# A projection kernel's result stores, and one load, moved from GpSimd's DMA queue to SyncE's

## The chip, the cores and the metric

The kernel runs as one program on the 8 cores of one Trainium2 chip. Each core takes 2048 of the 16384 tokens and works alone; nothing is exchanged. The metric is the device time in microseconds of the slowest core, from the runs of one kernel on one chip.

## The reference, cut to what matters

```python
x = x + layernorm(attn(layernorm(x)))       # x: 16384 tokens x 4096, float32
x = x + layernorm(ffn(layernorm(x)))

# attn, token by token: q, k, v are 64 heads x 64
q, k, v = x @ Wq.T, x @ Wk.T, x @ Wv.T      # q, k, v scaled by sigmoid masks
w = softmax(einsum('bshd,bsgd->bshg', q, k) / 8)    # heads against heads of one token
attn = einsum('bshg,bsgd->bshd', w, v).reshape(b, s, 4096) @ Wo.T

# ffn: a 4096x4096 base projection, and a top-2-of-8 LoRA of rank 16
ffn = x @ W_base.T + b_base + 2 * sum over the two chosen e of w_e * (x @ A_e.T) @ B_e.T
```

## The kernel before, in words

A core handles its tokens in two chunks of 1024 (`c` = 0, 1), each of 8 tiles (`tau`) of 128 tokens. One buffer in SBUF, `LNT`, holds the chunk transposed; the five 4096x4096 products (wq, wk, wv, wo, wb) all take their stationary operand from it and stream the weights through four buffers `WG0` to `WG3`.

One weight group is 512 rows by 512 columns in bf16 (512 KB), so a product has 8 column blocks `n` of 8 groups `ktg` each. `load_wgroup` (L240) fetches a group. The first time a weight is used (`cast_save`: in chunk 0, for wq, wk, wv and for the first half of wo and of wb) GpSimd issues the load from the float32 weight, cast on the way (`WG<-woT`, L247), and SyncE then issues a store of the bf16 group to a scratch tensor (`s_wo<-WG`, L250); the buffer is free for the next load when that store has landed and TensorE is done with it. Every later time (`scratch`) SyncE issues a plain load of the bf16 group (`WG<-s_wo`, L253). All of these run through the helper `dma` at L147/L148, so the trace gives them the line L148.

The stages of a chunk, in the order in which they are written out:

1. Layernorm of the 8 tiles and their transposes into `LNT` (`transpose_tile`, L278, evicted at L290 and L292).
2. q, k and v (L325 to L370): for each `n` 64 groups of matmuls into 8 banks (L343), then 8 evictions (L355, L361) and 8 stores of 128 KB from `QST` to `qn`, `kn`, `vn`, issued by SyncE.
3. Attention (`attn_batch`, L375): a tile is two batches; each gathers q, k, v in pieces of 128 bytes by 8 DMAs of SyncE (`QSG<-qn`, `KB<-kn`, `VB<-vn`), computes, and stores `OB` to `on` by 2 DMAs of SyncE (L537). After both batches of a tile, `a3_units` (L544) loads the tile of `on` into `BFN` (L549) and transposes it into `LNT`. Tiles 0 to 3 are done with all 8 banks before the projection begins.
4. wo, in two halves (`proj_half`, L575): tiles 0 to 3 in banks 0 to 3, with the attention of tiles 4 to 7 as a generator that is advanced three units after each group; then tiles 4 to 7, with the post-attention layernorm and the router (`a5_b0_units`, L619) of tiles 0 to 3. After each `n`, 4 evictions by ScalarE into the four slots of `APST` (L603) and 4 stores of 256 KB to `apn` (L607).
5. wb, in two halves (`b1_half`, L745): the same form, with a bias matmul (L778) and a LoRA matmul (L782) at the end of each `n`, 4 evictions (L787) and 4 stores to `yn` (L791). The final layernorm of tiles 0 to 3 (`b6_units`, L804) stands between the halves, that of tiles 4 to 7 at the end.

Nothing schedules this at run time: `emit` (L121) appends each instruction with its waits to the list of its engine, and each engine works through its list in order. So a DMA that must wait holds back whatever stands behind it on the engine that issues it. With four `WG` buffers, the load of group `ktg` waits for the matmuls of the group four before it.

Of the kernel before, what the change touches and what calls it, by code (L numbers as in the profile page):

```python
# [26 lines left out]
def _build_program():  # L27
# [24 lines left out]
    on_d = nc.dram_tensor("on", [CH, DM], BF16, kind="Internal").ap()  # L52
    ap_d = nc.dram_tensor("apn", [CH, DM], F32, kind="Internal").ap()
    yn_d = nc.dram_tensor("yn", [CH, DM], F32, kind="Internal").ap()
# [18 lines left out]
    BFN = sb("BFN", [128, DM], BF16)  # L73
# [73 lines left out]
    def dma(eng, out, in_, waits=(), sem=None):  # L147
        return emit(eng, lambda e, o=out, i=in_: e.dma_start(out=o, in_=i),  # L148
                    waits, inc=sem, amt=16)
# [147 lines left out]
    for c in range(NCH):  # L297
      try:
# [2 lines left out]
        src_kind0 = "cast_save" if c == 0 else "scratch"  # L301

        ph(1, c)
        lnt_rdy = {}
        for tau in range(TAU):
            xbuf, bname = (XT, "XT") if tau % 2 == 0 else (T2, "T2")
            lw = g_w(bname)
            if c == 0 and tau == 0:
                lw += [("setq", 48), ("G", g0)]
            qsem = "xl" if tau % 2 == 0 else "t2l"  # L310
            uq = dma("gpsimd", xbuf[:], x_d[row0 + tau * 128: row0 + tau * 128 + 128, :], lw,
                     sem=qsem)
            av = lnorm(xbuf[:], BFN[:], [(qsem, uq)] + g_w("BFN"))
            g_set(bname, ("V", av))
            fw = [("V", av)] + (g_w("LNTa", "LNTb") if tau == 0 else [])
            vv, ss = transpose_tile(BFN, lambda kt, tau=tau: colk(kt, tau), fw)
            lnt_rdy[tau] = [("V", vv), ("S", ss)]
            g_set("BFN", ("T", cnt["T"]))
        a1_v, a1_s = cnt["V"], cnt["S"]

# [4 lines left out]
        for nm in ("wq", "wk", "wv"):  # L325
            for n in range(NB):
                for ktg in range(8):
                    b, rdy = load_wgroup(nm, n, ktg, src_kind0)
                    for k4 in range(4):
                        kt = ktg * 4 + k4  # L330
                        for tau in range(TAU):
                            waits = []
                            if k4 == 0 and tau == 0:
                                waits.append(rdy)
                            if ktg == 0 and k4 == 0:
                                waits += g_w(f"bank{tau}")
                                if nm == "wq" and n == 0:
                                    waits += lnt_rdy[tau]
                            last = (ktg == 7 and k4 == 3)
                            emit("tensor",  # L340
                                 lambda e, kt=kt, tau=tau, b=b, k4=k4,
                                        st=(ktg == 0 and k4 == 0), sp=last:
                                 e.matmul(pb(tau, 0, 512),  # L343
                                          LNT[:, colk(kt, tau):colk(kt, tau) + 128],
                                          WG[b][:, k4 * 512:k4 * 512 + 512],
                                          start=st, stop=sp),
                                 waits, inc="T" if (k4 == 3 and tau == TAU - 1) else None)
                    wg_done(b, "T", cnt["T"])
# [195 lines left out]
        def a3_units(taus, wavesz, banks):  # L544
            for tau in taus:
                for bt in range(2):
                    yield from attn_batch(tau, bt, wavesz, banks)
                on_q = [("ob0", cnt["ob0"]), ("ob1", cnt["ob1"])]
                uq = dma("gpsimd", BFN[:], on_d[tau * 128:tau * 128 + 128, :],  # L549
                         list(on_q) + g_w("BFN"), sem="onr")  # L550
                lnt_key = "LNTa" if tau < 4 else "LNTb"
                fw = [("onr", uq)] + (g_w(lnt_key) if tau % 4 == 0 else [])
                yield
                transpose_tile(BFN, lambda kt, tau=tau: colk(kt, tau), fw, banks=banks)
                g_set("BFN", ("T", cnt["T"]))
                yield
# [18 lines left out]
        def proj_half(nm, taus, banks, src, gen, img_d, first_waits=()):  # L575
            for n in range(NB):
# [23 lines left out]
                for ti, tau in enumerate(taus):  # L600
                    sl = ap_i[0] % 4
                    ap_i[0] += 1
                    ev = emit("scalar", lambda e, bk=banks[ti], sl=sl: e.activation(  # L603
                        APST[:, sl * 512:sl * 512 + 512], pb(bk, 0, 512), AF.Copy),
                        ([("T", tmm)] if ti == 0 else []) + g_w(f"APs{sl}"), inc="S")
                    g_set(f"bank{banks[ti]}", ("S", ev))
                    uv = dma("gpsimd", img_d[tau * 128:tau * 128 + 128, 512 * n:512 * n + 512],  # L607
                             APST[:, sl * 512:sl * 512 + 512], [("S", ev)], sem=f"ap{sl}")
                    g_set(f"APs{sl}", (f"ap{sl}", uv))

# [134 lines left out]
        def b1_half(taus, banks, src, gen):  # L745
            for n in range(NB):
# [28 lines left out]
                for ti, tau in enumerate(taus):  # L775
# [12 lines left out]
                        APST[:, sl * 512:sl * 512 + 512], pb(bk, 0, 512), AF.Copy),  # L788
                        [("T", tmm)] + g_w(f"APs{sl}"), inc="S")
                    g_set(f"bank{banks[ti]}", ("S", ev))  # L790
                    uv = dma("gpsimd", yn_d[tau * 128:tau * 128 + 128, 512 * n:512 * n + 512],  # L791
                             APST[:, sl * 512:sl * 512 + 512], [("S", ev)], sem=f"ap{sl}")
                    g_set(f"APs{sl}", (f"ap{sl}", uv))
                g_set(f"bfTn{bfb}", ("T", cnt["T"]))
# [87 lines left out]
```

How the kernel before makes its waits and increments, by code:

```python
        def run(eng):  # L828
            for waits, fn, inc, amt in sched[name]:
                for s_, v_ in waits:
                    eng.wait_ge(sems[s_], v_)
                instr = fn(eng)
                if inc is not None:
                    instr.then_inc(sems[inc], amt)
```

## Time and profile before

| | us |
|---|---|
| runs of the kernel before | 8191.3, 8231.3, 8757.5 |
| median | 8231.3 |
| the profiled execution, device time | 8199.5 |
| its span, slowest core (core 1) | 8197.9 |
| spans of all cores | 8128.0 to 8197.9 |
| TensorE matmuls busy (core 1) | 5404.7 (66%) |
| weight loads busy | 2558.1 (31%) |
| VectorE busy | 1492.1 (18%) |
| ScalarE busy | 774.8 (9%) |
| GpSimd busy | 496.2 (6%) |
| DMA queue of GpSimd (q0), share of 16 engines | 26.8% |
| DMA queue of SyncE (q1), share of 16 engines | 23.3% |

The rows below are of core 1, in microseconds from the start of its span. Of the stages, chunk 0's q, k and v lie at about 130 to 1710, its attention and wo at 1710 to 3225, wb and the final layernorm at 3225 to 4250; chunk 1 has q, k and v at 4361 to about 5990, attention and wo to 7323, wb to 8079. A profile's row gives the busy time of a group of instructions and, in brackets, the idle time of the engine just before it with what ended it.

### The profile page before, as it was taken

What the parts mean: (1) busy time and instruction counts of PE and PEld (TensorE: products, weight loads), DVE (VectorE), ACT (ScalarE), POOL (GpSimd) and SP (SyncE); (2) the same over time, 40 slices, a digit from 0 to 9 for tenths busy, and PEclk for the clock granted to TensorE, in tenths of its full rate; (3) what the DMA queues carried; (4) which work ended last, traced back from release to release, by engine and by line L of the source; (5) the groups of instructions that cost most, each with busy time, mean ns of one, the idle gap of its engine ahead of it and who ended that gap; (6) DMA issues with size and microseconds to landing.
All of it is one profiled execution on the core that took longest, in us unless ns stands there. A gap on an engine that the chain in (4) does not pass through costs nothing.

```text
span 8197.9 us, 69969 instructions; the slowest of 8 cores (8128.0 to 8197.9 us)
## 1 busy us (share of the span) xinstructions
PE 5404.7 (66%) x28056; PEld 2558.1 (31%) x28056; DVE 1492.1 (18%) x2144; ACT 774.8 (9%) x1427; POOL 496.2 (6%) x785
## 2 busy tenths in 40 slices
PE   4888888842345457564917888888832565576864
PEld 2333333322222223221313333333322332233321
DVE  4000000023212251302042000000023222513012
ACT  1000000012112210000001000000012222100000
POOL 1000000000001000110100000000000000000010
PEclk7999999965677778787958999999965787788987
DMA  6666666632566655798552222222222443555655
GB/s 149 141 144 144 142 144 140 141 80 52 95 141 130 134 191 185 170 188 231 171 203 85 77 77 78 78 77 78 77 54 52 113 107 102 194 190 157 202 183 191
DMA packets 940079, 1084.79 MB, mean 132 GB/s; under 512 B 575217, under 2 KB 792306, under 8 KB 923378
## 3 DMA queue, kind: packets, MB, share of 16 engines
q0 software_dynamic: 225872, 492.98, 26.8%
q1 hardware_dynamic: 713890, 587.34, 23.3%
q8 instruction: 229, 3.75, 0.2%
q14 instruction: 88, 0.72, 0.0%
HBM read 885.23 MB, written 369.10 MB: 153 GB/s over the span
## 4 chain that ended last, share of the span: by engine, by line
PE 59%; DMA 15%; DVE 11%; ACT 6%; SPq 5%; issue 3%; POOL 1%; DVEq 0%; ACTq 0%; POOLq 0%
PE PALL L343 33%; PE PALL L592 11%; PE PALL L765 8%; SPq L148 5%; DVE BN L192 4%; DMA T<-yn 3%; DMA WG<-wbT 3%; ACT QBD L496 2%; ACT PSTG L472 2%; DMA VB<-vn 1%; PE PALL L278 1%; DMA WG<-woT 1%; PE PALL L489 1%; PE PALL L409 1%; DMA T<-apn 1%
## 5 line engine op out<-in xcount | busy, mean ns | idle before, releaser
L343 PE MATMUL PALL<-WG,LNT 128*128 128x512 bf16 x12288 | 2795.8, 389 | 407.9 <-DVE QST L361 109.3
L343 PEld LDWEIGHTS PALL<-WG,LNT 128*128 128x128 bf16 x12288 | 1224.2, 100 | 1978.8 <-issue 614.7
L592 PE MATMUL PALL<-WG,LNT 128*128 128x512 bf16 x4096 | 1034.3, 413 | 175.9 <-DMA WG<-woT 89.6
L765 PE MATMUL PALL<-WG,LNT 128*128 128x512 bf16 x4096 | 949.5, 393 | 133.9 <-DMA WG<-wbT 119.4
L278 PE MATMUL PALL<-idt,BFN 128*128 128x128 bf16 x1536 | 168.3, 307 | 825.2 <-DVE BFN L204 616.5
L592 PEld LDWEIGHTS PALL<-WG,LNT 128*128 128x128 bf16 x4096 | 418.9, 105 | 733.1 <-issue 355.3
L765 PEld LDWEIGHTS PALL<-WG,LNT 128*128 128x128 bf16 x4096 | 407.8, 101 | 663.0 <-issue 230.2
L192 DVE BATCH_NORM_STATS2 BN<-T 128x6 f32<-128x512 f32 x320 | 193.5, 675 | 1739.3 <-DMA T<-yn 1285.0
L361 DVE TENSOR_TENSOR QST<-PALL,maskK 128x512 bf16<-128x512 f32 x128 | 81.0, 684 | 2059.5 <-PE PALL L343 2017.0
L278 PEld LDWEIGHTS PALL<-idt,BFN 128*128 128x128 bf16 x1536 | 158.2, 145 | 840.2 <-issue 840.2
L437 ACT ACTIVATE KTS<-PALL 128x512 bf16<-128x512 f32 x192 | 104.2, 594 | 3048.1 <-PE PALL L429 3048.1
L409 PE MATMUL PALL<-idt,QSG 128*128 128x128 bf16 x1024 | 104.2, 273 | 328.7 <-DMA VB<-vn 321.5
L418 DVE CAST QBD<-PALL 128x512 bf16<-128x512 f32 x256 | 161.9, 684 | 745.8 <-PE PALL L409 745.8
L361 DVE TENSOR_TENSOR QST<-PALL,maskV 128x512 bf16<-128x512 f32 x128 | 80.9, 684 | 992.1 <-PE PALL L343 955.3
L489 PE MATMUL PALL<-idt,PSTG 128*128 128x128 bf16 x1024 | 101.8, 269 | 241.7 <-ACT PSTG L472 241.7
L409 PEld LDWEIGHTS PALL<-idt,QSG 128*128 128x128 bf16 x1024 | 89.4, 125 | 348.9 <-issue 337.8
L472 ACT ACTIVATE PSTG<-PALL,NM 64x512 bf16<-64x512 f32 x256 | 167.8, 679 | 285.0 <-DVE NM L466 162.4
L483 DVE TENSOR_REDUCE ZW<-PSTG 128x8 f32<-128x1024 bf16 (+1 forms) x96 | 151.2, 1575 | 199.9 <-ACT PSTG L472 199.9
L290 DVE CAST LNT<-PALL 128x512 bf16<-128x512 f32 x192 | 132.7, 691 | 272.2 <-PE PALL L278 271.8
L778 PE MATMUL PALL<-bbn,onesb 1*128 1x512 bf16 x128 | 51.4, 401 | 194.8 <-DMA bbn<-bb 194.8
L787 ACT ACTIVATE APST<-PALL 128x512 f32<-128x512 f32 x128 | 76.2, 597 | 1049.2 <-PE PALL L782 1045.2
L148 POOL DMA_DIRECT2D BFN<-on x16 | 8.6, 536 | 2702.9 <-DMA on<-OB 2702.9
(99 smaller groups left out, 2149.3 us busy)
## 6 DMA issues: line engine op xcount, KB each, us to landing
WG<-s_wo SPq DMA_DIRECT2D x192, 512.0 KB, 3.3
WG<-s_wb SPq DMA_DIRECT2D x192, 512.0 KB, 3.7
XT<-x POOLq DMA_DIRECT2D x24, 2048.0 KB, 11.6
WG<-wqT POOLq DMA_DIRECT2D x64, 512.0 KB, 5.9
s_wq<-WG SPq DMA_DIRECT2D x64, 512.0 KB, 3.6
WG<-wkT POOLq DMA_DIRECT2D x64, 512.0 KB, 5.6
s_wk<-WG SPq DMA_DIRECT2D x64, 512.0 KB, 3.1
WG<-wvT POOLq DMA_DIRECT2D x64, 512.0 KB, 5.7
```

The costliest lines, as they stand in the source:

```text
L148: return emit(eng, lambda e, o=out, i=in_: e.dma_start(out=o, in_=i), waits, inc=sem, amt=16)
L192: emit("vector", lambda e, i=i: e.bn_stats(BN[:, 6 * i:6 * i + 6], src_ap[:, 512 * i:512 * i + 512]), (list(vwaits) + g_w("MV") + g_w("BN" ...
L278: emit("tensor", lambda e, bk=bk, kt=kt, off=off: e.matmul(pb(bk, off * 128, 128), src_sb[:, kt * 128:kt * 128 + 128], idt[:], start=True, ...
L343: e.matmul(pb(tau, 0, 512), LNT[:, colk(kt, tau):colk(kt, tau) + 128], WG[b][:, k4 * 512:k4 * 512 + 512], start=st, stop=sp),
L361: ev = emit("vector", lambda e, tau=tau, sl=sl, mk=mk: e.tensor_tensor(QST[:, sl * 512:sl * 512 + 512].rearrange("p (h d) -> p h d", d=64) ...
L409: emit("tensor", lambda e, j=j, jj=jj, p=p, qb_bk=qb_bk: e.matmul(pb(qb_bk[j // 4], (j % 4) * 128, 128), QSG[p][:, jj * 128:jj * 128 + 128 ...
L418: emit("vector", lambda e, pw=pw, bk=bk, i_=i_: e.tensor_copy(QBD[pw][:, i_ * 512:i_ * 512 + 512], pb(bk, 0, 512)), [("T", t_s0)] if i_ == ...
L472: s_s6 = emit("scalar", lambda e, a=a, pw=pw, bk_i=bk_i, sb_=s_bk[bk_i]: e.activation(PSTG[pw][64 * a:64 * a + 64, bk_i * 1024:bk_i * 1024 ...
L489: emit("tensor", lambda e, j=j, pw=pw, ptb=pt_bk[j // 4], po=(j % 4) * 128: e.matmul(pb(ptb, po, 128), PSTG[pw][:, j * 128:j * 128 + 128], ...
L496: emit("scalar", lambda e, pw=pw, bk=bk, i_=i_: e.activation(QBD[pw][:, i_ * 512:i_ * 512 + 512], pb(bk, 0, 512), AF.Copy), [("T", t_s7)] ...
L592: e.matmul(pb(bk, 0, 512), LNT[:, colk(kt, tau):colk(kt, tau) + 128], WG[b][:, k4 * 512:k4 * 512 + 512], start=st, stop=sp),
L765: e.matmul(pb(bk, 0, 512), LNT[:, colk(kt, tau):colk(kt, tau) + 128], WG[b][:, k4 * 512:k4 * 512 + 512], start=st, stop=False), waits,
```

## The change

It has three parts.

- The load `BFN<-on` (L549; 16 of them), the stores `apn<-APST` (L607; 128) and the stores `yn<-APST` (L791; 128) are issued by SyncE and no longer by GpSimd.
- Their waits stay as they are, and so do sizes, buffers and semaphores.
- The first matmuls of wq in a chunk no longer wait tile by tile for the evictions of that tile's transposes; the matmul of tile 0 waits once, for all of them.

```diff
-            vv, ss = transpose_tile(BFN, lambda kt, tau=tau: colk(kt, tau), fw)
-            lnt_rdy[tau] = [("V", vv), ("S", ss)]
+            transpose_tile(BFN, lambda kt, tau=tau: colk(kt, tau), fw)
...
-                                if nm == "wq" and n == 0:
-                                    waits += lnt_rdy[tau]
+                                if nm == "wq" and n == 0 and tau == 0:
+                                    waits += [("V", a1_v), ("S", a1_s)]
...
-                uq = dma("gpsimd", BFN[:], on_d[tau * 128:tau * 128 + 128, :],
+                uq = dma("sync", BFN[:], on_d[tau * 128:tau * 128 + 128, :],
                          list(on_q) + g_w("BFN"), sem="onr")
...
-                    uv = dma("gpsimd", img_d[tau * 128:tau * 128 + 128, 512 * n:512 * n + 512],
+                    uv = dma("sync", img_d[tau * 128:tau * 128 + 128, 512 * n:512 * n + 512],
                              APST[:, sl * 512:sl * 512 + 512], [("S", ev)], sem=f"ap{sl}")
...
-                    uv = dma("gpsimd", yn_d[tau * 128:tau * 128 + 128, 512 * n:512 * n + 512],
+                    uv = dma("sync", yn_d[tau * 128:tau * 128 + 128, 512 * n:512 * n + 512],
                              APST[:, sl * 512:sl * 512 + 512], [("S", ev)], sem=f"ap{sl}")
```

On SyncE (SP), where chunk 0 goes from the first half of wo to the second, the order before was (`WG<-s_wo` is a load of a bf16 weight group, `apn<-APST` a store of results):

```order
L148 DMA s_wo<-WG 128x2048
L148 DMA on<-OB 64x32x64 x2
L148 DMA WG<-s_wo 128x2048 x64
L148 DMA s_wb<-WG 128x2048 x64
L148 DMA WG<-s_wb 128x2048 x64
```

and the same place of SyncE after the change is:

```order
L148 DMA s_wo<-WG 128x2048
L148 DMA apn<-APST 128x512 x4
L148 DMA on<-OB 64x32x64 x2
L148 DMA BFN<-on 128x4096
L148 DMA WG<-s_wo 128x2048 x8
L148 DMA apn<-APST 128x512 x4
L148 DMA WG<-s_wo 128x2048 x8
L148 DMA apn<-APST 128x512 x4
```

The 64 loads of a half now stand in eights, with the four stores of the block just computed between one eight and the next.

On GpSimd (POOL), from chunk 0's attention to its second column blocks of wo, the order before was (`WG<-woT` is the load of a float32 weight group with a cast):

```order
L148 DMA WG<-wvT 128x4x512 x64
L148 DMA BFN<-on 128x4096 x4
L148 DMA WG<-woT 128x4x512 x8
L148 DMA apn<-APST 128x512 x4
L148 DMA WG<-woT 128x4x512 x8
L148 DMA apn<-APST 128x512 x4
L148 DMA WG<-woT 128x4x512 x2
L148 DMA BFN<-on 128x4096
```

and after the change:

```order
L148 DMA WG<-wvT 128x4x512 x64
L148 DMA WG<-woT 128x4x512 x64
L148 DMA T<-apn 128x4096
L148 DMA XT<-x 128x4096
L148 DMA xp<-XT 128x4096
```

The 64 casting loads of the half now follow one another with nothing between them.

On SyncE, around the first tile boundary of the attention that is interleaved with chunk 0's wo (`QSG`, `KB`, `VB` are the gathers of the next batch), the order before was:

```order
L148 DMA on<-OB 64x32x64 x2
L148 DMA s_wo<-WG 128x2048
L148 DMA QSG<-qn 64x32x64 x2
L148 DMA KB<-kn 64x16x64 x4
L148 DMA VB<-vn 64x32x64 x2
L148 DMA s_wo<-WG 128x2048 x8
```

and after the change:

```order
L148 DMA on<-OB 64x32x64 x2
L148 DMA BFN<-on 128x4096
L148 DMA s_wo<-WG 128x2048
L148 DMA QSG<-qn 64x32x64 x2
L148 DMA KB<-kn 64x16x64 x4
L148 DMA VB<-vn 64x32x64 x2
L148 DMA s_wo<-WG 128x2048 x7
L148 DMA apn<-APST 128x512 x4
```

The load of `BFN`, which waits for the two stores of `OB` to land, now stands ahead of the next batch's gathers.

## Rows read from the trace of the kernel before

**Rows 1.** Spans and granted TensorE clock by core

```profile
core 1: 8197.9 us, clock 0.812
```

**Rows 2.** Who waited for whom: us in total, times, longest us

```profile
PE PALL L778 <- DMA bbn<-bb: 194.8, 2, 97.6
...
PE PALL L765 <- DMA WG<-wbT: 119.4, 37, 14.2
...
PE PALL L592 <- DMA WG<-woT: 89.6, 10, 12.9
PE PALL L343 <- DMA WG<-s_wv: 84.1, 8, 11.6
PE PALL L343 <- DMA WG<-s_wk: 82.8, 8, 11.7
...
PE PALL L343 <- DMA WG<-s_wq: 70.9, 7, 11.0
```

**Rows 3.** Timeline, chunk 1's wq, one block to the next: start, us, engine

```profile
4418.21 4.37 SPq L148 DMA_DIRECT2D qn<-QST  x8
...
4422.67 1.84 SPq L148 DMA_DIRECT2D WG<-s_wq  x4
4427.04 3.57 PE L343 MATMUL PALL<-WG,LNT 128*128 128x512 bf16 x8 [9.66 <-DMA WG<-s_wq]
```

**Rows 4.** Stretch behind it: us, PE, PEld, DVE, ACT, POOL busy, PEclk, DMA share, GB/s

```profile
4427.00:4430.40 3.40, 3.36 (x8) 1.24 (x9) 0.00 (x0) 0.00 (x0) 0.00 (x0) 0.50 0.82 333
```

**Rows 5.** Timeline, chunk 0's second half of wo, one block to the next

```profile
3046.80 2.07 ACT L603 ACTIVATE APST<-PALL 128x512 f32<-128x512 f32 x4 [28.90 <-PE PALL L592]
...
3047.54 4.65 PE L592 MATMUL PALL<-WG,LNT 128*128 128x512 bf16 x17 [0.89 <-ACT APST L603]
```

**Rows 6.** Timeline, chunk 1's first half of wb, one block to the next

```profile
7543.64 2.52 ACT L787 ACTIVATE APST<-PALL 128x512 f32<-128x512 f32 x4 [28.07 <-PE PALL L782]
```
```profile
7545.02 0.39 PE L782 MATMUL PALL<-bfTn,HWT 128*128 128x512 bf16 x1
...
7546.30 27.14 PE L765 MATMUL PALL<-WG,LNT 128*128 128x512 bf16 x125 [0.25 <-ACT APST L787]
```

**Rows 7.** Timeline, chunk 0's first half of wo, block 0 to 1

```profile
2222.10 3.02 POOL L148 DMA_DIRECT2D WG<-woT  x4
```

**Rows 8.** The same block boundary, TensorE's own timeline

```profile
2231.45 9.29 PE L592 MATMUL PALL<-WG,LNT 128*128 128x512 bf16 x32 [12.79 <-DMA WG<-woT]
```

**Rows 9.** Busy time and DMA, chunk 0's first half of wb (columns of rows 4)

```profile
3484.00:3772.00 288.00, 201.25 (x816) 81.26 (x814) 0.00 (x0) 13.36 (x23) 49.56 (x75) 0.86 0.93 195
```
```profile
3505.00:3510.00 5.00, 4.38 (x22) 1.82 (x20) 0.00 (x0) 0.00 (x0) 0.00 (x0) 1.00 1.12 246
```

**Rows 10.** Timeline, chunk 0's attention, tile 0 to tile 1, three engines

```profile
1815.04 3.96 SPq L148 DMA_DIRECT2D QSG<-qn  x2
```
```profile
1818.96 0.54 POOL L148 DMA_DIRECT2D BFN<-on  x1 [133.67 <-DMA on<-OB]
```
```profile
1833.08 1.78 PE L409 MATMUL PALL<-idt,QSG 128*128 128x128 bf16 x16 [3.53 <-DMA VB<-vn]
```

**Rows 11.** Timeline, chunk 0, tile 3's attention into wo, SyncE and TensorE

```profile
2117.29 1.70 SPq L148 DMA_DIRECT2D on<-OB  x2
...
2135.81 8.31 SPq L148 DMA_DIRECT2D QSG<-qn  x2
```
```profile
2162.43 1.01 PE L409 MATMUL PALL<-idt,QSG 128*128 128x128 bf16 x8 [21.36 <-DMA VB<-vn]
```

**Rows 12.** DMA issues between 2858 and 2880 us: KB each, median us to landing

```profile
BFN<-on POOLq DMA_DIRECT2D x1, 1024.0 KB, 10.7
```

**Rows 13.** DMA issues of the whole span (columns of rows 12)

```profile
WG<-s_wo SPq DMA_DIRECT2D x192, 512.0 KB, 3.3
```

**Rows 14.** Timeline, chunk 0, the last transposes' evictions and the first matmuls of wq

```profile
128.42 4.81 PE L343 MATMUL PALL<-WG,LNT 128*128 128x512 bf16 x18
128.72 0.59 ACT L292 CAST LNT<-PALL 128x512 bf16<-128x512 f32 x1 [0.27 <-PE PALL L278]
```

More of the change, by code:

```diff
@@ L303, in _build_program @@
         ph(1, c)
-        lnt_rdy = {}
         for tau in range(TAU):
```

## The prediction

> **What bounds the kernel now.** I began with the cores: all lie within 1%, and core 1 is the slowest [rows 1], so one core's queues tell the story. Its two totals of waits came next [rows 2]. The reader should see two things there. TensorE waits for scratch weights only in wq, wk and wv (70.9 + 82.8 + 84.1 = 237.8 us in 23 times, 10.3 us each): there the result stores already stand on SyncE ahead of the next loads. And in chunk 0 it waits for the casting loads of wo (89.6 us in 10 times) and wb (119.4 us in 37), where the stores stand on GpSimd ahead of the casting loads. Idle time of GpSimd and SyncE themselves costs nothing and I left it aside. Then I read the timeline at one boundary of each kind. TensorE with its weights bounds every projection, so the question at each block boundary (column block n to n+1) is which queue holds the next weights back.
>
> The change swaps the sides. Scratch projections of wo and wb, which today run through the boundary, get the stop that wq, wk and wv show; the two casting halves lose theirs.
>
> **Cost 1: block boundaries on scratch weights.** Today wo loses 0.89 us at a boundary [rows 5], and about 0.8 us more while three further banks are evicted at 0.5 us under matmuls of 0.22; wb loses 0.25 us [rows 6]. Afterwards SyncE reaches the next eight loads only after the last eviction and four stores. For wo the evictions run 2.07 us from 0.15 us after the last matmul [rows 5] and the last store takes about 0.5 us to issue (4.37 us for 8 [rows 3]), so the load is issued at 2.8 us. For wb the evictions keep pace with the L782 matmuls and end at 7546.16 [rows 6], 0.75 us after the last one ends at 7545.41: load issued at 1.3 us.
>
> From the first load's issue to the restart takes 4.4 us at the boundary of rows 3 (4422.67 to 4427.04). Its gap of 9.66 is 0.7 short of the mean of 23, which puts the leg at 5.0 on average. Here 1 MB of stores is in the queue within 2 us, not within 4.4, so I allow up to 1.5 more and take 0.5. The gap becomes 8.3 us in wo and 6.8 in wb; less what is lost today (1.7 and 0.25) that is 6.6 us each. Then the clock: behind the stop of rows 3 the eight matmuls take 3.57 us, with the granted clock at 0.50, its level of 1.2 GHz [rows 4]; at 2.4 GHz they take 8 x 0.217 (27.14 us for 125 [rows 6]) = 1.7. That adds 1.8 (3.57 less 1.74), so 8.4 us a boundary; I take 8.3, for a leg sometimes as short as in rows 3.
>
> Such boundaries: 7 in each of five half-products (wo second half and wb second half in both chunks, wb first half in chunk 1) = 35, x 8.3 = 290 us. Low end: the first load lands as fast as one in mid-block, 3.3 us [rows 13], with nothing ahead of it: 6.1 us a boundary (213 in all). High end: it waits for the whole megabyte, 3.1 us at the 333 GB/s of rows 4 less the 0.5 from last store to load, a leg of 7.6: 10.5 us (368). In chunk 1's first half of wo there are 7 more, but with attention in between TensorE is at half clock much of the time, so only the gap counts: 7 x 6.6 = 46 (35 to 60).
>
> The changes of half are hidden: behind wb's first half TensorE stands 97 us for `bbn<-bb`, which GpSimd reaches after the final layernorm [rows 2], and the weights are in long before. If that cover were gone, two more boundaries, 17 us.
>
> Where the load stands against the stores is weighed once more. In rows 3 a megabyte of stores was issued ahead of the load and it still started TensorE after 4.4 us. The Trainium skill ("DMA: Bandwidth & Descriptors", section Queues, rings and completion order) says that each DMA engine takes the descriptors of one issuing engine's ring in order, and alternates between the rings of two; by that rule the load, now in the stores' ring, waits for all that is left of them. By the row the sum has 290 us here, by the rule it would have 368. No row has stores of this size ahead of a load.
>
> **Cost 2: `BFN<-on` on SyncE.** Behind it stand the next batch's gathers. They are issued at 1815.04; `on` is seen as landed at 1818.96 [rows 10], so they start 4 us later, plus the load's own 1 MB, which already shares the engines today. TensorE waits 3.53 us for the gathers already. I take 3 us for each of 6 tile boundaries in the pure attention, 18 in all (6 to 30), and 19 for four in chunk 1's interleaved part (6 to 25), where the gathers today come just in time.
>
> **Cost 3: the single wait.** TensorE starts at 128.42, the last eviction ends at 128.72 + 0.59 = 129.31 [rows 14]: 1 us a chunk, 2 us.
>
> **Gain 1: chunk 0's first half of wo.** GpSimd issues `WG<-woT` at 2222.10, after evictions and stores, and TensorE restarts after 12.79 us [rows 7, 8]. Of the ten waits of rows 2 seven are of this kind and three short, so about 12.4 each. With the queue freed they fall to some 0.9: 7 x 11.5 = 80 us. SyncE's copy to scratch is then late by a few us, but its buffer is only needed four groups later (some 25 us with the attention between). Moreover the gathers of the next tile stand on SyncE behind `s_wo<-WG`, which waits for a casting load that GpSimd issues only after `BFN<-on`: they go out at 2135.81, 18.5 us after the stores of `OB` at 2117.29 [rows 11]. Now they go 6 us after them, and no longer beside four casting loads. That takes most of the 21.36 us gap, and 17, 11 and 7 at the next three tiles by the same reading: 56 together. 80 + 56 = 136; the casting loads now compete with the gathers inside the blocks, for which I take off 15: 121 us (80 to 136).
>
> **Gain 2: chunk 0's first half of wb.** The same order, but the DMA engines are busy 0.93 of the time [rows 9]. The 816 matmuls of those 288 us are six blocks of 136, 48 us each, with 44.6 us of DMA work. Packed as tightly as a full stretch (1.12 [rows 9]) it would take 40; I take 6.4 us a block, 45 in all (0 to 90, the latter if nearly the whole stop went, 7 x 12.8 as in rows 8).
>
> **Gain 3: end of the attention.** At 2860 `BFN<-on` needs 10.7 us [rows 12] because 4 MB of `T<-apn` and `XT<-x` are issued with it; these go out earlier now. 6 us a chunk, 12 (0 to 16).
>
> **Sum.** 290 + 46 + 18 + 19 + 2 - 121 - 45 - 12 = +197 us on the profiled execution's 8199.5: 8397 us, or 2.4% slower. That execution lies between the two lower runs (8191.3 and 8231.3), so it is a fair base.
>
> **Rivals.**
> - *Chunk 0 pays it back.* The casting halves lose their stops wholly and the scratch stops are short: cost 213 + 35 + 12 + 2 = 262, gain 136 + 90 + 16 = 242, so 8220 us, no slower. The place is GpSimd's queue in chunk 0. It decides from a gain of 213 us on, where the middle costs (375) leave 162 us, under 2%. For it: stops of 12 to 13 us are longer than those that arise. Against: there are 14 of them against 42, and rows 9 leave little DMA time in wb.
> - *The queue does not matter.* The loads and stores use the same engines whoever issues them; then only 272 issues move, none of which any engine waits for, and the time stays at 8200 us. Against it stand the 23 stops of wq, wk and wv, in the same form. The Trainium skill states this rule ("DMA: Bandwidth & Descriptors", section Issuing engines are not separate DMA queues: issuing from several engines saves only the sequencer's time to initiate); it says nothing of a wait ahead in the queue.
> - *Stores and loads collide.* The leg from issue to restart grows to 7 us or more because 1 MB of float32 is ahead on the same queue: 10.5 us a boundary, 368 + 60, and the gains fall to 150 as the casting halves get the same collisions: 8199.5 + 428 + 39 - 150 = 8517 us. For it: the stores are twice the size of those in rows 3. Against: the DMA engines have room even behind the restart, 0.82 [rows 4].
>
> **How the numbers follow.** My forecast has 0.55, chunk 0 paying back 0.20, the neutral queue 0.08, the collision 0.17. Two per cent (164 us) is about what a measurement of this kernel can tell from no change. The forecast's own spread reaches below 8364 about one time in ten (0.05 of its 0.55); slower is 0.50 + 0.17 = 0.67. The first two rivals are within 2% but for 0.04 of faster, should the tile boundaries in chunk 0 gain twice what I read: same is 0.05 + 0.16 + 0.08 = 0.29. The range runs from 8280, well into the first rival, to 8530, just over the third.
>
> **What would show it.** In the changed kernel's waits L592 and L765 should wait for `WG<-s_wo` and `WG<-s_wb` some 42 times at 7 to 8 us, and SyncE for ScalarE's `APST`. The waits of L592 for `WG<-woT` should nearly vanish, those of L765 for `WG<-wbT` shrink by a third, and the gap before L409 at chunk 0's tile 4 fall from 21 us to a few. Chunk 1 should lose about 240 us and chunk 0 gain about 45. It is wrong if L592 and L765 run through the scratch boundaries, or if chunk 0 gains over 210 us.

## The result, and the profile after

The changed kernel took 8654.2 us in the median of 10 runs, the kernel before 8402.1 us in 10 runs on the same chip. The ratio is 1.0262, 95% interval 1.0232 to 1.0291: slower, by 2.6% where 2.4% was forecast. Some executions of either kernel have the cores of one die at a lower granted clock and take several per cent longer, which the ratio leaves out and the medians don't; cores 0 to 3 of the profiled execution after are such cores, so core 5 is read here, in both traces. The forecast of 8397 us, and its range up to 8530, lie below the median of 8654.2. Spans and clock of the changed kernel:

```profile
core 1: 8499.3 us, clock 0.795
...
core 5: 8404.2 us, clock 0.807
```

and the kernel before, the same core:

```profile
core 5: 8167.1 us, clock 0.814
```

That is 237 us more, 2.9% of this core's span. TensorE's waits of the changed kernel (us in total, times, longest):

```profile
PE PALL L590 <- DMA WG<-s_wo: 216.2, 28, 15.7
...
PE PALL L763 <- DMA WG<-s_wb: 168.6, 25, 8.9
...
PE PALL L763 <- DMA WG<-wbT: 73.7, 40, 5.0
```

and the same of the kernel before, core 5, which answer to [rows 2]:

```profile
PE PALL L765 <- DMA WG<-wbT: 120.7, 37, 14.4
...
PE PALL L592 <- DMA WG<-woT: 87.7, 9, 13.1
...
PE PALL L592 <- DMA WG<-s_wo: 60.0, 8, 16.1
...
PE PALL L765 <- DMA WG<-s_wb: 8.1, 4, 2.8
```

(Lines behind the first edit stand two lower after the change: L592 is L590, L765 is L763.) The wait for `WG<-woT` is gone from the list, that for `WG<-wbT` is 47 us shorter, and 317 us of waits for scratch weights have come. One boundary of chunk 0's second half of wo, which answers to [rows 5], from the timeline (start, us, engine; in brackets the idle time before and what ended it):

```profile
3033.57 2.07 ACT L601 ACTIVATE APST<-PALL 128x512 f32<-128x512 f32 x4 [35.18 <-PE PALL L590]
3034.24 1.79 SPq L148 DMA_DIRECT2D apn<-APST  x4
3036.12 17.68 SPq L148 DMA_DIRECT2D WG<-s_wo  x7
3040.77 13.50 PE L590 MATMUL PALL<-WG,LNT 128*128 128x512 bf16 x52 [7.36 <-DMA WG<-s_wo]
```

The reader sees the chain in its order: evictions, four stores, and only then the loads, 2.7 us after the last matmul (3033.41); TensorE starts 4.65 us behind their issue. The same at a boundary of chunk 1's first half of wb, which answers to [rows 6]:

```profile
7635.17 2.24 SPq L148 DMA_DIRECT2D yn<-APST  x4
7637.50 2.25 SPq L148 DMA_DIRECT2D WG<-s_wb  x4
7643.73 16.46 PE L763 MATMUL PALL<-WG,LNT 128*128 128x512 bf16 x62 [7.47 <-DMA WG<-s_wb]
```

In the first stop and behind both, busy times by stretch (us, PE, PEld, DVE, ACT, POOL, granted clock, DMA share, GB/s):

```profile
3036.10:3040.70 4.60, 0.00 (x0) 0.00 (x0) 0.00 (x0) 0.00 (x0) 0.00 (x0) 0.74 1.01 319
...
3040.70:3044.20 3.50, 3.43 (x9) 1.33 (x10) 0.00 (x0) 0.00 (x0) 0.00 (x0) 0.50 0.90 366
...
7647.20:7650.30 3.10, 3.10 (x10) 1.09 (x9) 0.00 (x0) 0.00 (x0) 0.00 (x0) 0.60 0.00 0
7650.30:7665.00 14.70, 14.70 (x70) 6.67 (x69) 0.00 (x0) 0.00 (x0) 0.00 (x0) 1.00 0.44 143
```

After an idle time of 7.4 us TensorE works at 0.50 of its clock (1.2 GHz). At this boundary of wo it is back at 2.4 GHz 4.3 us after the restart (granted clock 0.50 from 3040.77 to 3045.09, then 1.00), at that of wb 5.9 us after it (7643.73 to 7649.67; the 0.60 above is the mean of a stretch with the change of level in it).

Stage by stage, from TensorE's timeline of core 5 (how much longer each stage lasts than before; x4_late and x5_mixed are kernels of the experiments):

| stage | change | x1_apn | x2_yn | x3_bfn | x4_late | x5_mixed |
|---|---|---|---|---|---|---|
| c0 attention, tiles 0-3 | +14 | +3 | +9 | +20 | +22 | +8 |
| c0 wo, first half with attention | -92 | -56 | +5 | -23 | -84 | -59 |
| c0 wo, second half, blocks 1-7 | +55 | +55 | 0 | 0 | 0 | 0 |
| c0 wb, first half, block 0 | +13 | -4 | +7 | +6 | -4 | +11 |
| c0 wb, first half, blocks 1-7 | -41 | 0 | -39 | +3 | -39 | -44 |
| c0 wb, second half, blocks 1-7 | +62 | 0 | +64 | 0 | -1 | 0 |
| c1 attention, tiles 0-3 | +2 | +3 | +4 | +3 | +5 | +6 |
| c1 wo, first half with attention | +50 | +38 | +2 | +15 | +3 | +4 |
| c1 wo, second half, blocks 1-7 | +55 | +55 | 0 | 0 | 0 | 0 |
| c1 wb, first half, blocks 1-7 | +64 | +2 | +65 | +2 | 0 | 0 |
| c1 wb, second half, blocks 1-7 | +63 | 0 | +63 | -2 | -1 | -1 |

The projections without attention repeat mostly to 1 or 2 us where nothing was edited, at most to 4; the stages with attention, block 0 of a half and the layernorms scatter by up to some 15 us. Chunk 1 pays 233 us (forecast 240); chunk 0 comes out at +4, where a gain of 45 was forecast. The changes of half stay hidden, as forecast: the second half of wb begins 5 us (chunk 0) and 9 us (chunk 1) later after the end of the first, and its block 0, with the wait for `bbn<-bb` in it, is 9 and 11 us shorter.

### The profile page after: what moved, and what is told of

The parts are those of the page before. It is cut to its first block, busy times and chain, and to the rows that moved or that the text cites. A ratio compares the mean times of both kernels' runs of the same rounds, so it can differ in the third digit from the quotient of the medians.

```text
span 8543.4 us, 69964 instructions; the slowest of 8 cores (8365.6 to 8543.4 us)
## 1 busy us (share of the span) xinstructions
PE 5572.6 (65%) x28056; PEld 2602.3 (30%) x28056; DVE 1493.0 (17%) x2144; ACT 774.9 (9%) x1427; POOL 348.1 (4%) x513
## 4 chain that ended last, share of the span: by engine, by line
PE 57%; DMA 18%; DVE 11%; ACT 6%; SPq 5%; issue 3%; POOL 0%; DVEq 0%; ACTq 0%; POOLq 0%
PE PALL L341 32%; PE PALL L590 10%; PE PALL L763 9%; SPq L148 5%; DVE BN L192 3%; DMA WG<-wbT 3%; DMA T<-yn 3%; DMA WG<-s_wo 2%; DMA VB<-vn 2%; DMA WG<-s_wb 2%; ACT QBD L494 2%; ACT PSTG L470 2%; PE PALL L278 1%; DMA s_wb<-WG 1%; PE PALL L487 1%
## 5 line engine op out<-in xcount | busy, mean ns | idle before, releaser
L341 PE MATMUL PALL<-WG,LNT 128*128 128x512 bf16 x12288 | 2800.6, 390 | 401.6 <-DVE QST L359 109.8
L341 PEld LDWEIGHTS PALL<-WG,LNT 128*128 128x128 bf16 x12288 | 1225.0, 100 | 1976.7 <-issue 615.9
L763 PE MATMUL PALL<-WG,LNT 128*128 128x512 bf16 x4096 | 1070.3, 430 | 259.6 <-DMA WG<-s_wb 182.8
L590 PE MATMUL PALL<-WG,LNT 128*128 128x512 bf16 x4096 | 1062.4, 423 | 230.7 <-DMA WG<-s_wo 220.8
L763 PEld LDWEIGHTS PALL<-WG,LNT 128*128 128x128 bf16 x4096 | 437.0, 108 | 881.4 <-issue 677.5
L590 PEld LDWEIGHTS PALL<-WG,LNT 128*128 128x128 bf16 x4096 | 428.2, 107 | 806.4 <-issue 443.6
L506 PE MATMUL PALL<-VB,QBD 128*128 128x64 bf16 x1024 | 63.1, 226 | 158.9 <-ACT QBD L494 158.9
```

What stands on the lines that cost most here:

```text
L341: e.matmul(pb(tau, 0, 512), LNT[:, colk(kt, tau):colk(kt, tau) + 128], WG[b][:, k4 * 512:k4 * 512 + 512], start=st, stop=sp),
L590: e.matmul(pb(bk, 0, 512), LNT[:, colk(kt, tau):colk(kt, tau) + 128], WG[b][:, k4 * 512:k4 * 512 + 512], start=st, stop=sp),
L763: e.matmul(pb(bk, 0, 512), LNT[:, colk(kt, tau):colk(kt, tau) + 128], WG[b][:, k4 * 512:k4 * 512 + 512], start=st, stop=False), waits,
```

## The experiments

The theory is the prediction's: a load stands behind the stores of the block just computed on the engine that issues both, and waits for their evictions. The rivals: stores and loads collide in the DMA engines whatever their order; or the queue does not matter. All edits below are to the kernel before or the changed one as named. Where stores of one kernel are divided over two engines, each engine's stores count on semaphores of their own.

**x4_late.** The changed kernel with all stores still on SyncE, but behind the first four loads of the next block:

```diff
                     b, rdy = load_wgroup(nm, n, ktg, src)
+                    if ktg == 3:
+                        flush_late(late)
...
-                    uv = dma("sync", img_d[tau * 128:tau * 128 + 128, 512 * n:512 * n + 512],
-                             APST[:, sl * 512:sl * 512 + 512], [("S", ev)], sem=f"ap{sl}")
-                    g_set(f"APs{sl}", (f"ap{sl}", uv))
+                    late.append((img_d[tau * 128:tau * 128 + 128, 512 * n:512 * n + 512], sl, ev))
+            flush_late(late)
```

`flush_late` issues the listed stores; `b1_half` has the same edit for `yn`.

> The changed kernel, all stores still issued by SyncE, but those of a block stand behind the first four loads of the next block and no longer ahead of them. Theory (the order on the issuing engine makes the stop): the 42 stops vanish, the waits of L590 and L763 for scratch weights return to those of the kernel before, chunk 0 keeps its gain; about 8199 - 90 - 41 + 30 = 8100 us, ratio 0.988 (0.982 to 0.994). Rival (megabytes of stores and loads in one ring collide, whatever the order): still above 1.01. Rival (SyncE is overloaded with issues): still above 1.01.

Measured: ratio 0.9835 (0.9733 to 0.9937), core 5 at 8068.3 us. Its timeline at a boundary of chunk 0's second half of wo, SyncE and TensorE:

```profile
2989.76 10.68 SPq L148 DMA_DIRECT2D WG<-s_wo  x4
3000.87 2.53 SPq L148 DMA_DIRECT2D apn<-APST  x4
```
```profile
3000.94 28.61 PE L601 MATMUL PALL<-WG,LNT 128*128 128x512 bf16 x128 [0.90 <-ACT APST L612]
```

The loads go out during the block before, the stores at the same moment as ever, and the stop is 0.90 us, as in [rows 5]. The same 256 stores share the same queue with the same loads, and the table's five stages of +55 to +64 are at 0 or -1, while chunk 0's gains stay. What costs is the order on the issuing engine; that the queue does not matter at all is refuted by x1_apn and x2_yn below. The collision is not ruled out by this run alone, since the first four loads now also move their data before the stores do. The changed kernel's own trace prices it: at its 35 boundaries on scratch weights without attention the first load lands 4.4 to 7.4 us after its issue, 5.3 in the mean, and TensorE restarts 5.6 us after it, where that rival had 7 us or more; the last three loads of a block land after 3.2 us in the median. So some 2 of the 8 to 9 us are the company of the stores and of the loads issued together with it (no run parts these two); the rest is the late issue, a load's own time and the slow clock.

**x9_one.** x4_late with one load ahead of the stores in place of four, in both projections:

```diff
-                    if ktg == 3:
+                    if ktg == 0:
                         flush_late(late)
```

> The kernel with the stores on SyncE but late, with one load of the next block ahead of the four stores in place of four. Theory (the stop is the wait for the evictions plus the issue of four stores plus the leg of a load, 2.7 + 4.7 us as the changed kernel's boundary shows): the first load goes out early and feeds TensorE for 16 matmuls, 3.5 us, after a restart at 0.9 us; the second load is issued 2.8 us after the last matmul and lands 4.7 us later, at 7.5, when TensorE has been dry since 4.4: about 3 us at each of 42 boundaries, 126 us more than with four loads ahead, so about 30 us slower than the kernel before (ratio 1.003). Rival A (one load ahead is enough, because the stores cost nothing once TensorE has been restarted): ratio 0.984 as with four. Rival B (the second load waits for all the bytes of the stores, whichever load is first): 6 us a boundary, ratio 1.02.

Measured: no ratio could be formed. Cores 0 to 3 of the profile, which are read here, have spans of 8199.5 to 8245.5 us, 48 to 72 us more than the same cores before (core 1, read below, 8245.5 against 8197.9 [rows 1]); expected were about 30. A boundary, core 1:

```profile
2974.02 4.43 PE L601 MATMUL PALL<-WG,LNT 128*128 128x512 bf16 x16 [0.89 <-ACT APST L612]
2982.64 17.67 PE L601 MATMUL PALL<-WG,LNT 128*128 128x512 bf16 x68 [4.19 <-DMA WG<-s_wo]
```
```profile
2973.95 2.17 SPq L148 DMA_DIRECT2D apn<-APST  x4
2976.21 2.64 SPq L148 DMA_DIRECT2D WG<-s_wo  x4
```

TensorE restarts after 0.89 us on the one group it has, and runs dry until the second has landed: the restart comes 6.4 us after its issue here. Over this half's seven boundaries the second gap is 2.5 to 4.2 us, mean 3.4 (expected 3), and the 112 matmuls behind it take 24.3 to 27.2 us, where 24.3 is the full clock; the stage is 35 us longer than before, 5.0 a boundary. Rival A (one load is enough) and rival B (6 us a boundary) are both out. The dose works: no load ahead of the stores costs 8 to 9 us a boundary, one 4 to 5, four nothing.

**x1_apn and x2_yn.** The kernel before with only the stores of wo on SyncE (x1_apn, shown), or only those of wb (x2_yn, the same edit at `yn_d`):

```diff
-                    uv = dma("gpsimd", img_d[tau * 128:tau * 128 + 128, 512 * n:512 * n + 512],
+                    uv = dma("sync", img_d[tau * 128:tau * 128 + 128, 512 * n:512 * n + 512],
```

> The kernel before with only the 128 stores apn<-APST on SyncE (under semaphores of their own); yn<-APST, BFN<-on and the first waits of wq as before. Theory (the stores' place ahead of the scratch loads costs about 8 us a boundary): wo's 14 boundaries in the two second halves +110 us, chunk 1's first half +40, chunk 0's first half -80 since its casting loads no longer stand behind the stores; together +70 us, ratio 1.009 (1.004 to 1.014). Rival (the queue does not matter): 1.000, no waits of wo for WG<-s_wo beyond those of before. Rival (the load of BFN is what costs): 1.000 or below.

> The kernel before with only the 128 stores yn<-APST on SyncE. Theory: wb's 21 scratch boundaries at 9.2 us = +193 us, chunk 0's first half -41; together about +150 us, ratio 1.018 (1.013 to 1.023), the larger part of the change's loss. Rival (the queue does not matter): 1.000.

Measured: x1_apn 1.0100 (0.9993 to 1.0208), x2_yn 1.0142 (1.0037 to 1.0247). The first interval reaches 1, so the whole time alone would not show x1_apn's loss; the stages do. By them each has its own boundaries' cost: wo 55/7 = 7.9 us, wb 64/7 = 9.1 us a boundary. Each also has its own casting half's gain, -56 (expected -80) and -39 (expected -41).

**x3_bfn and x13_stores.** x3_bfn is the kernel before with only `BFN<-on` on SyncE, and the single wait; x13_stores is the changed kernel with only `BFN<-on` given back to GpSimd:

```diff
-                uq = dma("sync", BFN[:], on_d[tau * 128:tau * 128 + 128, :],
+                uq = dma("gpsimd", BFN[:], on_d[tau * 128:tau * 128 + 128, :],
```

(x3_bfn has the same two lines the other way round.)

> The changed kernel with apn<-APST and yn<-APST back on GpSimd: what is left of the change is BFN<-on on SyncE and the single wait of wq. Theory: +20 us or less (about 2.5 us at each of 6 tile boundaries of the pure attention, 4 to 5 at four of chunk 1's interleaved ones, 2 us for the wait, less some us in chunk 0 where casting loads no longer stand behind it), ratio 1.000 to 1.003. Rival (BFN<-on ahead of the gathers carries the loss): 1.01 or more.

> The changed kernel with only the load BFN<-on given back to GpSimd: all 256 result stores stay on SyncE, the single wait stays. It asks what the term for BFN<-on (37 us of cost, part of the 56 us gained at chunk 0's tile boundaries) is worth. Theory, from the one-part runs (BFN alone: chunk 0's pure attention +20 us, its interleaved attention -23 us, chunk 1's interleaved attention +15 us): the two sides nearly cancel, and the kernel stays within 15 us of the changed one, ratio 1.025 to 1.027 to the kernel before; the pure attention of chunk 0 is 14 to 20 us shorter than in the changed kernel, chunk 0's first half of wo some 30 us longer. Rival (the prediction's own terms): 18 + 19 us of cost go and some 30 us of gain, as forecast, ratio 1.022 to 1.027; they part by the stages: by this one chunk 1's interleaved attention is 19 us shorter too and the pure attention of both chunks 9 us shorter each.

Measured: neither run allowed a ratio, so core 5 is compared. x3_bfn's took 8206.7 us, 40 more than before, but 29 of these are in two stages that the edit does not touch (15.3 at wb's second half, block 0, in chunk 0, 13.8 from there to chunk 1). x13_stores' core 5 took 8386.4 against the changed kernel's 8404.2, its cores 4 to 7 8381.9 to 8418.9 against 8365.6 to 8404.2: on the whole time the load's place makes no difference that these show. The stages of core 5 show two sides. With `BFN<-on` on SyncE chunk 0's pure attention is 17 us longer (14.3 against -2.3), chunk 1's interleaved part 13 us longer (49.7 against 36.4), and chunk 0's first half of wo 29 us shorter (-92.1 against -62.6). Theory and prediction had the same sign everywhere; the pure attention of chunk 1, for which the prediction's own terms had 9 us, shows 1.

**x5_mixed.** The kernel before with only the casting halves' stores on SyncE, in both projections:

```diff
-                    uv = dma("gpsimd", img_d[tau * 128:tau * 128 + 128, 512 * n:512 * n + 512],
-                             APST[:, sl * 512:sl * 512 + 512], [("S", ev)], sem=f"ap{sl}")
+                    sq, asem = ("sync", f"ay{sl}") if src == "cast_save" else ("gpsimd", f"ap{sl}")
+                    uv = dma(sq, img_d[tau * 128:tau * 128 + 128, 512 * n:512 * n + 512],
+                             APST[:, sl * 512:sl * 512 + 512], [("S", ev)], sem=asem)
```

> The kernel before, with only the result stores of the two casting halves (chunk 0's first half of wo and of wb) moved to SyncE; the five and more halves on scratch weights keep theirs on GpSimd, and BFN<-on stays there too. Theory (each queue's order sets the stop): both gains of the change and none of its costs. From the stages of the one-part runs: chunk 0's first half of wo 56 us shorter, its first half of wb 39 us shorter, nothing at the 42 scratch boundaries: about 95 us faster on the profiled execution, a ratio of 0.988. Rival (the gain in chunk 0 is bought from the same DMA work elsewhere): these halves stay as long as before and the ratio is 1.00.

Measured: 0.9886 (0.9840 to 0.9931), where 0.988 was expected. The stages are in the table: -59 and -44, and nothing at the scratch boundaries. Core 5 of the profile is only 65 us below before, not 95: stages that the edit does not touch are each some us longer in this execution. The rule is simple: a store belongs on the engine that is not issuing the next loads, or behind those loads (x4_late).

**x6_qkv.** The change turned round: the kernel before with chunk 1's stores of `qn`, `kn` and `vn` on GpSimd:

```diff
-                    qv = dma("sync", img[nm][tau * 128:tau * 128 + 128, 512 * n:512 * n + 512],
+                    sq, qsm = ("gpsimd", f"qg{sl}") if c == 1 else ("sync", f"qs{sl}")
+                    qv = dma(sq, img[nm][tau * 128:tau * 128 + 128, 512 * n:512 * n + 512],
```

> The kernel before, with chunk 1's 192 stores of qn, kn and vn moved from SyncE to GpSimd: the change turned round, at the boundaries that stop today. Theory: the 23 waits for scratch weights at 10.3 us go, and what is left is the wait for the evictions of banks 4 to 7, which need the four slots of QST freed by stores that land some 3 us after issue: 4 to 5 us a boundary. 23 x 5 to 6 = 115 to 140 us faster, ratio 0.983 to 0.986. Rival (the four slots or the number of the stores set these stops, not the queue): the gaps stay near 10 us, now as waits for the banks, ratio 1.00 or, as GpSimd issues a store more slowly, 1.00 to 1.01.

Measured: 0.9819 (0.9765 to 0.9873). The stage is 132 us shorter, 5.7 us a boundary. Before and then this kernel, TensorE in chunk 1's wq, core 5:

```profile
4592.80 57.54 PE L343 MATMUL PALL<-WG,LNT 128*128 128x512 bf16 x255 [9.93 <-DMA WG<-s_wq]
```
```profile
4588.66 1.85 PE L343 MATMUL PALL<-WG,LNT 128*128 128x512 bf16 x4 [0.89 <-ACT QST L355]
4592.69 56.70 PE L343 MATMUL PALL<-WG,LNT 128*128 128x512 bf16 x252 [2.19 <-ACT QST L355]
```

The wait for the weights is gone, and the next one behind it is seen: after four matmuls TensorE waits for the fifth bank, whose eviction waits for a slot of `QST`.

**x10_all.** x4_late, and in chunk 1's wq, wk and wv the next block's first four loads ahead of the evictions and stores:

```diff
                 tmm = cnt["T"]
+                if c == 1 and (nm, n) != ("wv", NB - 1):
+                    nx = (nm, n + 1) if n + 1 < NB else ({"wq": "wk", "wk": "wv"}[nm], 0)
+                    pre = [load_wgroup(nx[0], nx[1], kg, src_kind0) for kg in range(4)]
```

> The kernel with all stores on SyncE but late (four loads of the next block ahead), and the same done at chunk 1's wq, wk and wv: the next block's first four loads stand ahead of the evictions' eight stores. Theory: the 42 stops stay away (99 us faster than before), and the 23 stops of wq, wk and wv fall from 10.3 us to 4 to 5, what the four slots of QST leave, with a little clock regained: 23 x 6 to 7 = 140 to 160 us more. About 250 us faster than the kernel before, ratio 0.969. Rival (the stops of wq, wk and wv are set by the slots of QST and the evictions): no more than the late stores gave, ratio 0.984 to 0.988.

Measured: no ratio could be formed; the spans of the cores are 7902.8 to 7979.6 us (before: 8128.0 to 8197.9), core 5's is 249 us less than before (about 250 expected). The stage of q, k and v is 142 us shorter, at the low end of the expected 140 to 160, with the same 2.2 us gap at the fifth bank as x6_qkv; so its stores' place, GpSimd or late on SyncE, hardly matters.

**x11_tiles.** x10_all with `BFN<-on` of tiles 0 to 3 on GpSimd, on SyncE only where the attention is interleaved.

```diff
-                uq = dma("sync", BFN[:], on_d[tau * 128:tau * 128 + 128, :],
-                         list(on_q) + g_w("BFN"), sem="onr")
+                gq = tau < 4
+                uq = dma("gpsimd" if gq else "sync", BFN[:], on_d[tau * 128:tau * 128 + 128, :],
+                         list(on_q) + g_w("BFN"), sem="onr2" if gq else "onr")
```

> The kernel with late stores everywhere (also in chunk 1's wq, wk, wv), with BFN<-on of tiles 0 to 3 of both chunks back on GpSimd, and on SyncE only where the attention is interleaved. Theory (behind BFN<-on on SyncE stand the gathers of the next batch): the 20 us that chunk 0's pure attention lost come back, chunk 1's gives 0 to 5, the rest stays: 15 to 25 us faster than the kernel with late stores everywhere, ratio 0.966 to 0.972. Rival (those 20 us are scatter from one execution to the next, and not the queue): no difference in that stage.

Measured: 0.9695 (0.9624 to 0.9766), core 5 at 7887.2 us, 31 less than x10_all (expected 15 to 25). Chunk 0's pure attention goes from +21.5 to -4.7 against before. In x10_all, SyncE there:

```profile
1820.79 1.68 SPq L148 DMA_DIRECT2D on<-OB  x2
1825.72 0.34 SPq L148 DMA_DIRECT2D BFN<-on  x1
1826.14 5.57 SPq L148 DMA_DIRECT2D QSG<-qn  x2
```

The gathers go out 5.3 us after the stores of `OB`, since SyncE stands at `BFN<-on` until `on` has landed. The cost of a load that waits, ahead of loads that needn't, is shown by x13_stores and x11_tiles both, in the same stage.

**x12_slots.** x11_tiles with eight slots for the evictions of wq, wk and wv:

```diff
-                    sl = qst_i[0] % 4
+                    sl = qst_i[0] % 8
+                    QB, so = (QST, sl) if sl < 4 else (OB[0], sl - 4)
```

> The same, with eight slots for the evictions of wq, wk and wv in place of four (the second four in OB, which is idle in that stage). Theory: what is left of the stops of chunk 1's wq, wk and wv after the loads went ahead of the stores (about 4 us a boundary: 0.89 for the first bank, then waits for banks 4 to 7) is the wait of the evictions for slots; with eight slots it falls to some 2 us as at wo's boundaries: 23 x 2 = 46 us in chunk 1, and 23 x 1 to 2 = 23 to 46 in chunk 0, where four slots stop the evictions too: 70 to 90 us faster than the same kernel with four slots, ratio 0.957 to 0.961. Rival (the evictions themselves, 0.5 us each on one engine, set what is left): no difference, 0.966 to 0.972.

Measured: 0.9431 (0.9390 to 0.9471), core 5 at 7686.8 us: the fastest, 5.7% below the kernel before. The step from x11_tiles is 200 us, not the 70 to 90 expected: 60 in chunk 1, 154 in chunk 0, less 15 by which its interleaved attention in chunk 1 is longer. The kernel before, chunk 0's wq at one boundary, shows what the 1 to 2 us expected there had passed over:

```profile
387.28 1.84 PE L343 MATMUL PALL<-WG,LNT 128*128 128x512 bf16 x4 [0.89 <-ACT QST L355]
390.26 0.38 PE L343 MATMUL PALL<-WG,LNT 128*128 128x512 bf16 x1 [1.14 <-ACT QST L355]
395.31 0.59 PE L343 MATMUL PALL<-WG,LNT 128*128 128x512 bf16 x1 [4.67 <-ACT QST L355]
396.22 54.09 PE L343 MATMUL PALL<-WG,LNT 128*128 128x512 bf16 x243 [0.33 <-ACT QST L355]
```

and x12_slots there:

```profile
363.99 57.33 PE L342 MATMUL PALL<-WG,LNT 128*128 128x512 bf16 x256 [0.89 <-ACT QST L358]
```

Four gaps (0.89 + 1.14 + 4.67 + 0.33 = 7.0 us) have become one of 0.89. The slots set them; in the waits of before they are spread over two rows of L343, for `QST` of VectorE and of ScalarE, that look small beside the waits for weights. The rival (the evictions' own speed) is out.

## Why the prediction was right, and where it was wrong

The mechanism and the relative loss were right. The absolute time failed at its base, and among the terms Gain 1 and Gain 2 were put too high; both are taken up below.

- **What bounds each boundary: right.** 317 us of waits for scratch weights came, in 53 less 12 = 41 times more (42 forecast), behind SyncE's stores; those for `WG<-woT` went. x4_late shows that the order on SyncE is the cause, as it takes them away by this order alone.
- **Cost 1, 290 us: right.** Five half-products give 55.2 + 62.4 + 55.0 + 64.4 + 63.0 = 300.0. The gap in chunk 0's second half of wo is 7.95 us in the mean of seven (forecast 8.3), that in wb's three halves 7.2 to 7.3 (6.8). The slow clock cost wb some 2 us and lasts 5.9 us at the boundary shown, not only for the first eight matmuls as the 1.8 us assumed; so wb came to 9.1 a boundary and wo to 7.9, around the 8.3. Chunk 1's first half of wo lost 36.4 us in x13_stores, where only its stores were moved, and 38.2 in x1_apn; forecast 46, of which the gap alone was priced.
- **Stores ahead of the load.** The first load started TensorE 4.65 us after its issue at the boundary shown, 5.2 us in the mean of that half and 5.6 us in the mean of all 35 (forecast 5.5 with the share of the stores, 7.6 at the high end). That 5.5 came out by luck: the 5.0 in it, worked out from the mean gap, was a misreading, as the 23 legs of the kernel before (core 1) are 4.6 us in the mean, and the stores' share was 1 us and not 0.5. At the boundary shown, from the first load's issue to the restart, the DMA engines were busy the whole time, at 319 GB/s, and from the first store's issue to the restart 6.5 us passed, in which 1.5 MB can go at 240 GB/s. So a load that waits for all the stores ahead of it could also have landed then, and the landings say the same: at each of the 35 boundaries the load landed 0.6 us or more after the last store (here 4.4 us after the load's issue, the store 2.8 us after it). The rule of the Trainium skill ("DMA: Bandwidth & Descriptors", section Queues, rings and completion order), that each DMA engine takes the descriptors of a ring in order, agrees with these landings. What failed is the price that the prediction gave it, 368 us: it added the whole megabyte from the last store on to a leg in which stores were running already.
- **The neutral queue: wrong, as given little chance.** With the rule of the Trainium skill ("DMA: Bandwidth & Descriptors", section Issuing engines are not separate DMA queues), that all issuing engines use the same DMA engines, x4_late agrees (the stores on SyncE cost nothing there). x1_apn with x4_late shows what the rule leaves out: 8 to 9 us a boundary from waits that stand ahead in the issuing engine's order.
- **Cost 2, 18 + 19 us: right in total, not in place.** x13_stores against the changed kernel has 17 + 1 in the pure attention and 13 in chunk 1's interleaved part. Why chunk 1's pure attention is spared was not tried.
- **Gain 1, 121 us: mis-sized, it was 92.** Its first part holds: the stops of 12 us fell to 0.84 to 0.90 and x13_stores and x1_apn, with the stores alone, have 62.6 and 56.0 (80 less 15 was forecast). The step of this term that failed is "That takes most of the 21.36 us gap, and 17, 11 and 7 at the next three tiles by the same reading: 56 together": `BFN<-on` added 29 us. At tile 4 the gap fell from 21.05 us to

```profile
2158.66 1.01 PE L407 MATMUL PALL<-idt,QSG 128*128 128x128 bf16 x8 [9.83 <-DMA VB<-vn]
```

and not to a few; and at the next tile `on` itself lands late, 11.6 us after its second store was issued (4.7 at tile 4). SyncE after the change:

```profile
2292.10 1.76 SPq L148 DMA_DIRECT2D on<-OB  x2
2304.44 0.33 SPq L148 DMA_DIRECT2D BFN<-on  x1
2304.86 0.38 SPq L148 DMA_DIRECT2D s_wo<-WG  x1
2305.33 6.69 SPq L148 DMA_DIRECT2D QSG<-qn  x2
```

The gathers go 13.2 us after the stores of `OB`, not the 6 us read off for tile 4 (there 2128.61 to 2134.95, 6.3). The casting loads now run through; that it is they that hold up these small stores I take from the order of events, and no run tests it.
- **Gain 2, 45 us: mis-sized, it was 28 in this execution, 41 without block 0.** Blocks 1 to 7 gained 41, and x5_mixed and x13_stores 44 and 43; block 0 lost 13 in this execution and 7 and 11 in x2_yn and x5_mixed, but gained 4 or 5 in x4_late and x13_stores, so I put it down to scatter.
- **Gain 3, 12 us: right.** 7.6 and 4.4 at the stage's next mark. **Cost 3** is too small to be seen (0.0 at the first matmul of wq in chunk 0).
- **Sum and absolute time.** The sum was 197 and the difference on core 5 is 237: 29 us less of gain 1, 17 less of gain 2, 10 more of cost 1, 15 less in chunk 1's interleaved wo (50 for 46 + 19), 4 less of costs 2 and 3, together 37, and the rest scatter. The ratio forecast, 1.024, lies inside the measured interval, closer than the terms deserve: their errors partly cancel, and core 5 alone has 2.9%.
- **The absolute time: wrong.** The step that failed is "That execution lies between the two lower runs (8191.3 and 8231.3), so it is a fair base". The median of ten runs before is 8402.1 us, 2.5% above the 8199.5 taken, and a forecast of 1.024 times that median would have been 8604 against the 8654.2 measured. The fastest run after the change took 8415.0 us, 0.2% over the forecast. The 8757.5 us in the table of runs had shown how far single runs lie above such an execution; the range should have reached up for it.
- **"Chunk 0 pays it back": wrong in size.** Chunk 0 gained 133 us at its casting halves, not 213 or more, and paid 118 in its own two scratch halves.

## What to carry to other kernels

Read, for each stage, which engine issues the loads that are needed next, and keep off that engine every DMA that waits for a result, or write it behind those loads; where sources change from stage to stage, so does the right engine (x5_mixed). A stop at a boundary hides the next: when the load was moved in chunk 1, the slots of the staging buffer came out (60 us), and in chunk 0 they had stood there all along (154 us); together they were worth 200 us, nearly what the whole change had cost. Small waits of the kind "four matmuls, a gap, one matmul, a gap" should be added up by boundary, since no group of waits shows their sum.

## What the runs showed that I had not expected

- A load wave with one group in hand still loses 4 to 5 us a boundary (x9_one): 3.4 us of gap, and most of the rest is slow clock behind it.
- Four slots for eight evictions cost 6.7 us a boundary in chunk 0 (154/23), beside casting loads, and 2.6 us (60/23) in chunk 1, beside plain loads.
- The stores' issue itself is not what holds the loads: 4 issues take 1.79 us, while the evictions that they wait for take 2.07 us and run at the same time.
